# The slot-update tail of a fused attention and slot-routing block: three values products in split form, transposes under a sum, and the first output tiles one place earlier

## What is computed

```
alpha = softmax of the 8 largest routing logits of a row, 0 elsewhere   # [rows, 64]
S_new = gated update of the slots from alpha^T x                          # [64, 512] per sequence
q, k, v = S_new wq + bq, S_new wk + bk, S_new wv + bv
y   = S_new + softmax(q k^T * scale) v
y   = layernorm(y) * ln_g + ln_b
out = x + (alpha (y wvp + bvp)) wo + bo
```

## Time and profile before

| | |
|---|---|
| median of three runs | 371.1 us (370.83 to 371.25) |
| the profiled execution's own time | 370.99 us |
| its span, first to last instruction | 369.1 us |
| mean granted clock of TensorE | 0.997 |
| busy: PE, DVE, ACT, POOL | 350.7, 243.5, 188.2, 194.1 us |
| output tiles | 32 transfers of 256 KB, issued from 340.95 to 365.02 us |

### The profile page before, as it was taken

The page is one execution under the profiler, slowest core; times in us unless marked ns, Lnnn a source line. Parts: engine busy times, 40 slices in busy tenths (PEclk is TensorE's granted clock), DMA queues, the critical chain, the costliest instruction groups (busy, mean ns, idle before and its releaser), DMA issues.

```text
span 369.1 us, 6877 instructions
## 1 busy us (share of the span) xinstructions
PE 350.7 (95%) x2250; PEld 273.4 (74%) x2250; DVE 243.5 (66%) x718; ACT 188.2 (51%) x394; POOL 194.1 (53%) x344
## 2 busy tenths in 40 slices
PE   5999999999999999999999999999999999999881
PEld 2475658999998898898988989867556785657651
DVE  0839986877788787787887786765372433366673
ACT  1260035568669577587496594665232342244541
POOL 1317056888776786677678568440021151215882
PEclk9999999999999999999999999999999999999998
DMA  5889966242232312323131100079000000000778
GB/s 170 271 290 365 387 175 189 72 115 90 83 115 61 113 60 86 88 62 111 59 115 59 31 2 2 0 233 315 3 0 0 2 0 0 3 0 0 282 299 330
DMA packets 41366, 42.78 MB, mean 116 GB/s; under 512 B 3678, under 2 KB 32478, under 8 KB 41331
## 3 DMA queue, kind: packets, MB, share of 16 engines
q1 hardware_dynamic: 39376, 40.42, 33.1%
q10 hardware_dynamic: 1666, 1.27, 1.2%
q0 software_dynamic: 288, 0.66, 0.7%
HBM read 32.18 MB, written 8.39 MB: 110 GB/s over the span
## 4 chain that ended last, share of the span: by engine, by line
PE 72%; DVE 10%; POOL 6%; issue 4%; ACT 4%; DMA 3%; SPq 0%; DVEq 0%; POOLq 0%; ACTq 0%
PE psum L328 11%; PE psum L329 10%; PE psum L330 10%; PE psum L1344 8%; PE psum L1394 5%; PE psum L1554 4%; PE psum L1597 3%; PE psum L1240 3%; PE psum L1422 3%; PE psum L1615 2%; PE psum L1282 2%; DMA WvpT<-in_WvpT 2%; PE psum L1375 2%; PE psum L1541 2%; POOL X L474 2%
## 5 line engine op out<-in xcount | busy, mean ns | idle before, releaser
L328 PE MATMUL psum<-GW_hi,hT_hi 128*128 128x292 f32 (+1 forms) x256 | 79.0, 308 | 1.1 <-POOL GW_lo L456 1.0
L330 PE MATMUL psum<-GW_lo,hT_hi 128*128 128x292 f32 (+1 forms) x256 | 74.0, 289 | 0.0
L329 PE MATMUL psum<-GW_hi,hT_lo 128*128 128x292 f32 (+1 forms) x256 | 73.9, 288 | 0.0
L474 POOL TENSOR_TENSOR X<-X,th 128x512 f32<-128x512 f32 x32 | 38.3, 1196 | 31.5 <-ACT th L1062 31.5
L328 PEld LDWEIGHTS psum<-GW_hi,hT_hi 128*128 128x128 f32 x256 | 48.4, 189 | 2.9 <-issue 2.0
L469 POOL TENSOR_TENSOR hT_lo<-xT,hT_hi 128x512 fp32r<-128x512 f32 x32 | 43.4, 1356 | 11.9 <-ACT hT_hi L1018 11.9
L329 PEld LDWEIGHTS psum<-GW_hi,hT_lo 128*128 128x128 f32 x256 | 48.3, 189 | 0.2 <-issue 0.2
L330 PEld LDWEIGHTS psum<-GW_lo,hT_hi 128*128 128x128 f32 x256 | 48.1, 188 | 0.0
L328 PE MATMUL psum<-xhT_hi,w_hi 128*128 128x256 f32 x128 | 38.4, 300 | 0.1
L329 PE MATMUL psum<-xhT_hi,w_lo 128*128 128x256 f32 x128 | 36.1, 282 | 0.0
L330 PE MATMUL psum<-xhT_lo,w_hi 128*128 128x256 f32 x128 | 36.0, 282 | 0.0
(11 more groups left out here) (247 smaller groups left out, 820.6 us busy)
## 6 DMA issues: line engine op xcount, KB each, us to landing
X<-in_x SPq DMA_DIRECT2D x32, 256.0 KB, 3.5
xT<-in_xT SPq DMA_DIRECT2D x32, 256.0 KB, 2.7
out<-ost SPq DMA_DIRECT2D x32, 256.0 KB, 2.8
WhhT<-in_WhhT SPq DMA_DIRECT2D x1, 3072.0 KB, 12.5
WihT<-in_WihT SPq DMA_DIRECT2D x4, 768.0 KB, 7.8
WvpT<-in_WvpT SPq DMA_DIRECT2D x4, 256.0 KB, 5.5
Wo<-in_wo ACTq DMA_DIRECT2D x4, 256.0 KB, 3.7
WaT<-in_WaT SPq DMA_DIRECT2D x1, 1024.0 KB
```

The lines of the kernel that those rows point to most:

```text
L328: pe.matmul(out, w_hi, m_hi, start=start, stop=False)
L329: pe.matmul(out, w_lo, m_hi, start=False, stop=False)
L330: return pe.matmul(out, w_hi, m_lo, start=False, stop=stop)
L474: pool.tensor_tensor(tile_x(r), tile_x(r), halves(th[:, :]), ALU.add).then_inc(S("x2"), 1)
```

## The change

The values of pairs 1 to 3 are computed with `mm3` from split halves: `Wv_hi`, `Wv_lo` (2048 columns each) and `SnT_hi`, `SnT_lo` (128 x 4 x 384). ACT makes the upper halves, DVE the lower ones. They lie over the gate weights `WihT` and under the buffers of `SV_hi`, `SV_lo`, `al_hi` and `al_lo`, so ACT's first cast waits for the late gates, and `high_alpha` now waits for the last values product. In `y_of` the slots are turned back by four true transposes, put ahead of the attention product and its waits. `values(3)` is cut in two around `y_turned(0)`. `low_y` of pairs 0 and 1 goes from DVE to POOL. PE runs outs 0 and 1 ahead of `values_of(1)`, outs 2 and 3 behind it, and `y_turned(3)`, `values_of(2)`, outs 4 and 5, `values_of(3)`, and the rest follow. From outs 6 on, three pairs of banks are used in turn. Tile 2 goes from POOL to DVE. Two pairs of semaphores early in the kernel become one each; nothing else changes there.

```diff
+    Wv_hi = place("Wv_hi", [P, KC, D], F32R, "v1")       # v1: over WihT, same start as c1
+    Wv_lo = place("Wv_lo", [P, KC, D], F32R, "v1")
+    SnT_hi = place("SnT_hi", [P, KC, VN], F32R, "v1")
...
-        return OB2[m % 2]
+        return OB2[m % 2] if m < 6 else OB2[(2, 0, 1)[m % 3]]
...
-        return n % 3 == 2
+        return n > 4 and n % 3 == 2
...  POOL
-        low_alpha(0)
-        low_alpha(1)
         scales_y(0)
         scales_y(1)
+        low_y(0)
         scales_y(2)
+        low_alpha(0)
+        low_y(1)
         low_slot_values(0)
         scales_y(3)
         low_y(2)
+        low_alpha(1)
         low_slot_values(1)
-        out(2)
+        out(5)
         low_y(3)
-        out(5)
         low_alpha(2)
+        low_slot_values(2)
         out(8)
         out(11)
-        low_slot_values(2)
-        out(14)
+        low_slot_values(3)
         low_alpha(3)
-        out(17)
-        low_slot_values(3)
-        for n in range(20, NT, 3):
+        for n in range(14, NT, 3):
...  DVE
+        low_values_weight()
         late_new_slots()
+        low_slots(V1, EN, 2)
+        low_slots(EN, SLOTS, 3)
         scores(0, EP, 1)
...
+        stats_y(2)
         weights_turned(EP, NPAIR, 2)
-        low_y(0)
-        stats_y(2)
         norm_y(2)
-        low_y(1)
         slot_values(0)
         stats_y(3)
+        outs(0)
         norm_y(3)
+        outs(1)
         slot_values(1)
-        for m in range(6):
-            outs(m)
+        outs(2)
+        outs(3)
+        outs(4)
         slot_values(2)
-        for m in (6, 7):
-            outs(m)
+        outs(5)
         slot_values(3)
...  ACT
         def high_alpha(g):
-            act.wait_ge(S("gi_late"), 3)
+            act.wait_ge(S("v"), NPAIR)
...
+        high_values_weight()
         act.wait_ge(S("gn_in"), KC + 1)
...
+        high_slots(V1, EN)
         query_key(0, EN, 0)
+        act.wait_ge(S("snt"), KC + 1)
+        high_slots(EN, SLOTS)
         exps(0, EP, 1)
-        high_alpha(0)
-        high_alpha(1)
         query_key(EN, SLOTS, 2)
         exps(EP, NPAIR, 2)
+        high_alpha(0)
         turned_y(0)
         turned_y(1)
+        high_alpha(1)
         high_slot_values(0)
         turned_y(2)
         high_slot_values(1)
-        scaled_out(2)
+        scaled_out(5)
         turned_y(3)
-        scaled_out(5)
         high_alpha(2)
+        high_slot_values(2)
         scaled_out(8)
         scaled_out(11)
-        high_slot_values(2)
-        scaled_out(14)
+        high_slot_values(3)
         high_alpha(3)
...  PE
+                    last = mm3(pe, VB[g], SnT_hi[:, k, at_g], SnT_lo[:, k, at_g], Wv_hi[:, k, :], Wv_lo[:, k, :],
+                               k == 0, k == KC - 1)
...
-            pe.matmul(yb, atT[:, g, :], V[:, g, :], start=True, stop=True)
             for c in range(KC):
-                last = pe.matmul(yb[:, c * P:(c + 1) * P], SnT[:, c, g * P:(g + 1) * P], ident[:, :],
-                                 start=False, stop=c == KC - 1, skip_group_check=True)
+                pe.matmul(yb[:, c * P:(c + 1) * P], SnT[:, c, g * P:(g + 1) * P], ident[:, :], start=c == 0, stop=False,
+                          is_transpose=True, skip_group_check=True)
+            pe.wait_ge(S("atT"), 1 + g // EP)
+            pe.wait_ge(S("vs"), g + 1)
+            pe.matmul(yb, atT[:, g, :], V[:, g, :], start=False, stop=True, skip_group_check=True).then_inc(S("y"), 1)
...
-        values(3)
+        values(3, 0, 2)
         y_turned(0)
+        values(3, 2, KC)
...
         y_turned(2)
-        values_of(1)
         outs(0)
         outs(1)
+        values_of(1)
+        outs(2)
+        outs(3)
         y_turned(3)
-        for m in (2, 3, 4, 5):
-            outs(m)
         values_of(2)
-        outs(6)
-        outs(7)
+        outs(4)
+        outs(5)
         values_of(3)
-        for m in range(8, NT // 2):
+        for m in range(6, NT // 2):
             outs(m)
```

More of the change, by code:

```diff
@@ L103, in program @@
     blockmask = place("blockmask", [P, P], F32, "b1")
+    V1, VN = P, SLOTS - P
+    region("v1", cursor["x"])
+    Wv_hi = place("Wv_hi", [P, KC, D], F32R, "v1")
+    Wv_lo = place("Wv_lo", [P, KC, D], F32R, "v1")
+    SnT_hi = place("SnT_hi", [P, KC, VN], F32R, "v1")
     region("c1", cursor["x"])
@@ L177, in program @@
     alT = place("alT", [P, NPAIR * TPB, P], F32, "keep")
+    region("v2", cursor["keep"])
+    SnT_lo = place("SnT_lo", [P, KC, VN], F32R, "v2")
     region("c4", cursor["keep"])
@@ L278, in program @@
     YT = (banks[0], banks[1], banks[0], banks[0])
-    OB2 = ((banks[2], H0), (banks[1], H1))
+    OB2 = ((banks[2], H0), (banks[1], H1), (banks[0], SI))
     def out_banks(m):
-        return OB2[m % 2]
+        return OB2[m % 2] if m < 6 else OB2[(2, 0, 1)[m % 3]]
     def out_tile(n):
@@ L530, in low_y @@
             pool.wait_ge(S("yhi"), g + 1)
-            pool.wait_ge(S("ylo"), g)
             pool.tensor_tensor(ynT_lo[:, g % 2, :, :], ynT[:, g % 2, :, :], ynT_hi[:, g % 2, :, :].bitcast(F32),
@@ L644, in _ @@
         v.wait_ge(S("encWT"), KC)
-        v.wait_ge(S("gall"), 1)
+        v.wait_ge(S("gauss"), 2)
         with v.If(f > 0):
@@ L652, in _ @@
                 v.wait_ge(S("u_out"), i + 2)
-        v.tensor_copy(flagf[:, :], anyv[:, 0:1]).then_inc(S("u_done"), 1)
+        v.tensor_copy(flagf[:, :], anyv[:, 0:1]).then_inc(S("first_row"), 1)
         stats1(0)
         v.wait_ge(S("pre"), HB_DONE)
-        v.tensor_tensor(hb[:, :], banks[0][:, 0:HC], b1, ALU.add).then_inc(S("hb"), 1)
+        v.tensor_tensor(hb[:, :], banks[0][:, 0:HC], b1, ALU.add).then_inc(S("first_row"), 1)
         link(v.tensor_tensor(brz[:, 0:2 * KC], bih[:, 0:2 * KC], bhh[:, 0:2 * KC], ALU.add), "rt")
@@ L674, in _ @@
         stats1(2)
-        v.wait_ge(S("gw"), 1)
+        v.wait_ge(S("gauss"), 1)
         link(v.tensor_scalar(gw[0:WP, :], gw[0:WP, :], geo[:, 1:2], None, ALU.max), "rt")
@@ L919, in norm_y, with low_values_weight, low_slots @@
             v.wait_ge(S("yn"), g + 1)
[L921 to L924, removed]
+        def low_values_weight():
+            v.wait_ge(S("vhi"), 1)
+            v.tensor_tensor(Wv_lo[:, :, :], Wv[:, :, :], Wv_hi[:, :, :].bitcast(F32), ALU.subtract).then_inc(S("vlo"), 1)
+        def low_slots(lo, hi, n):
+            v.wait_ge(S("vhi"), n)
+            at_s = slice(lo - V1, hi - V1)
+            v.tensor_tensor(SnT_lo[:, :, at_s], SnT[:, :, lo:hi], SnT_hi[:, :, at_s].bitcast(F32),
+                            ALU.subtract).then_inc(S("vlo"), 1)
         def slot_values(g):
@@ L999, in _ @@
         act.wait_ge(S("dist"), 2)
-        act.activation(gw[0:WP, :], wcl[0:WP, :], ACT.Exp, scale=-1.0 / DEV).then_inc(S("gw"), 1)
+        act.activation(gw[0:WP, :], wcl[0:WP, :], ACT.Exp, scale=-1.0 / DEV).then_inc(S("gauss"), 1)
         link(act.activation(gall[:, :], gall[:, :], ACT.Exp, scale=-1.0 / DEV))
-        act.mul(gall[:, :], gall[:, :], 1.0 / T).then_inc(S("gall"), 1)
+        act.mul(gall[:, :], gall[:, :], 1.0 / T).then_inc(S("gauss"), 1)
         act.wait_ge(S("in_wa"), 16)
@@ L1191, in high_alpha, with high_values_weight, high_slots @@
             act.copy(al_hi[:, g % 2, :, :], alT[:, TPB * g:TPB * (g + 1), :]).then_inc(S("al_hi"), 1)
+        def high_values_weight():
+            act.wait_ge(S("in_v"), 48)
+            act.wait_ge(S("gi_late"), 3)
+            act.copy(Wv_hi[:, :, :], Wv[:, :, :]).then_inc(S("vhi"), 1)
+        def high_slots(lo, hi):
+            act.copy(SnT_hi[:, :, lo - V1:hi - V1], SnT[:, :, lo:hi]).then_inc(S("vhi"), 1)
         def scaled_out(n):
@@ L1220, in _ @@
         high_slot_values(1)
-        scaled_out(2)
+        scaled_out(5)
         turned_y(3)
-        scaled_out(5)
         high_alpha(2)
+        high_slot_values(2)
         scaled_out(8)
         scaled_out(11)
-        high_slot_values(2)
-        scaled_out(14)
+        high_slot_values(3)
         high_alpha(3)
-        scaled_out(17)
-        high_slot_values(3)
-        for n in range(20, NT, 3):
+        for n in range(14, NT, 3):
             scaled_out(n)
@@ L1259, in _ @@
         last.then_inc(S("pre"), 1)
-        pe.wait_ge(S("gall"), 1)
+        pe.wait_ge(S("gauss"), 2)
         pe.wait_ge(S("flag"), 1)
@@ L1274, in _ @@
                 pe.sem_inc(S("u_read"), 1)
-        pe.wait_ge(S("u_done"), 1)
+        pe.wait_ge(S("first_row"), 1)
         pe.wait_ge(S("encWT"), KC)
@@ L1286, in _ @@
         pe.wait_ge(S("wcs"), 2)
-        pe.wait_ge(S("hb"), 1)
+        pe.wait_ge(S("first_row"), 2)
         pe.matmul(banks[0], cmean[:, :], wcs[:, :], start=True, stop=True).then_inc(S("pre"), 1)
@@ L1548, in scores, with values @@
             last.then_inc(S("ss"), 1)
-        def values(g):
+        def values(g, lo=0, hi=KC):
             if g > 1:
                 pe.wait_ge(S("vs"), g - 1)
-            for k in range(KC):
-                last = pe.matmul(VB[g], SnT[:, k, g * P:(g + 1) * P], Wv[:, k, :], start=k == 0, stop=k == KC - 1)
-            last.then_inc(S("v"), 1)
```

(24 more changed lines are left out.)

2 lines of the change are left out of this document (removed).

## The result

The changed kernel takes 373.96 us, median of four runs (373.71 to 374.05); the kernel before, beside it, 371.12 (370.83 to 371.25). The ratio is 1.0077, 95% interval [1.0059, 1.0094]: slower by 0.8%. The profiled execution took 373.9, with a span of 372.1 and a mean granted clock of 0.986. The direction and the place are as predicted. The time is 1.6 us above the forecast of 372.4, since one term of the sum was sized wrong: it lies outside the 371.8 to 373.3 that the forecast gave its own case, and inside the whole range, 370.0 to 374.0, by 0.04. That it still lies inside is luck.

What follows compares the result with a forecast made beforehand. The prediction took SP's in-order output queue, standing at POOL's tile 8, as the bound: 351.55 + 0.96 lead + 24 tiles at 0.64 (15.35) + 1.0 hole + 1.66 + 1.89 = 372.4 us. Range 370.0 to 374.0.

Steps and rivals of the forecast that it cites:

- its own case: Whole kernel: in-order queue behind tile 8 sets the end, 372.4 us, range 371.8 to 373.3, chance 0.49.
- What bounds the kernel: Output drain: the tile POOL finishes at which SP's queue stands last, plus 0.64 us for each tile behind it.
- the same sum: End of kernel: SP's issue time, 0.96 us lead, 0.64 per remaining tile, 1.66 from dry queue to span end.
- PE sets the end: Rival for the kernel's end: all 3.6 us of saved PE work come through, 367.4 us; chance 0.17.
- The savings on PE: PE: split values save 0.6 us for each of three pairs, transposes 0.44 in each of four; 3.6 in all.
- the rival in which these forms give nothing: Values and turned slots on PE: products stay 3.43, turns 0.89, 374.8 us; shares 0.08 with two other rivals.
- The split halves were hidden: Making the halves on ACT and DVE early: cost taken as zero; without cover, under 1 us.
- The added wait: PE ahead of `values_of(0)`: `high_alpha(0)` holds back `turned_y(0)` on ACT, so start is 330.5, only 0.8 earlier than before.
- The order on POOL: `low_slot_values(2)` now ahead of tile 8, so tile 8 is finished at 351.5, against SP's issue at 348.53 before.
- Tile 14's hole: Output drain: tile 14 reaches SP at 356.4, transfers run dry once, adding 1.0 us.
- `values_of(0)` at 2.82: PE's twelve f32r products for pair 0's slot values: taken at 2.82 us, as in the kernel before.
- this rival, at 2.8 us: PE's wait before `values_of(0)` drops TensorE's clock to 1.2 GHz: 2.8 us more, 375.2; shares 0.08 with two others.

Runs made afterwards that it cites:

- e1: Changed kernel with ACT's cast `high_alpha(0)` moved behind `turned_y(0)`; 370.58 us, ratio 0.9987 to the kernel before.
- e2: Changed kernel with two f32 products that nobody reads added on PE inside its wait ahead of `values_of(0)`; 372.16 us, ratio 1.0023 to the kernel before.
- e6: Changed kernel with the values of pairs 1 to 3 in plain f32 again, without split halves; 371.71 us, ratio 1.0012 to the kernel before.
- e7: Changed kernel with slots turned back by plain f32 products against the identity instead of transposes; 372.63 us, ratio 1.0041 to the kernel before.
- e9: e7 with two more casts of pair 0's `alT` on ACT, so PE waits longer; 375.32 us, ratio 1.0099 to the kernel before.
- e10: Changed kernel, transposes kept, with `low_y(0)` on DVE again; 371.42 us, ratio 1.0012 to the kernel before.
- e12: Changed kernel with tile 8 alone finished by DVE; 371.99 us, ratio 1.0029 to the kernel before.
- e3: Changed kernel with tiles 8 and 14 finished by DVE instead of ACT and POOL; 371.31 us, ratio 0.9983 to the kernel before.
- e8: Kernel before with only the transposes in `y_of`, put ahead of the attention product; 369.57 us, ratio 0.9955 to the kernel before.
- e4: e1 with tiles 8, 11 and 14 finished by DVE; 367.79 us, ratio 0.9916 to the kernel before.
- e5: Kernel before with only `low_slot_values(2)` moved ahead of tiles 8 and 11 on POOL; 372.75 us, ratio 1.0042 to the kernel before.

## Why the prediction was right, and where it was off

**What bounds the kernel: right.** The end follows from SP's issue of tile 14 in the changed kernel, to 0.1 us. With the issue times of the table the same sum gives the spans of e1, e2, e6, e7, e9, e10 and e12 to 0.1 as well. Moving tiles 8 and 14 to DVE (e3) gives 2.3 us back with `values_of(0)` as slow. The rival "PE sets the end" (367.4) falls: e2 and e6 add work to PE and are faster. PE's work counts as far as it brings those tiles forward, as in e8. The third pair of banks, tile 2 on DVE and PE's new order of outs were given nothing, and no run takes one of them alone; e4, which keeps all three, is faster than the kernel before.

**The savings on PE: right in size.** Two pairs' values took 5.65 (5.64), and four transposes 0.44 from one start to the next piece's (319.45 to 319.89; 0.45 in the sum). So the rival in which these forms give nothing falls too. The split halves were hidden, as taken: by the timelines PE's values of pair 1 started between 311.24 and 311.69 in the runs that have the halves, and between 311.42 and 311.68 in those without, so no cost of theirs shows.

**The added wait: right.** Pair 0's rows came to PE at 324.47 (forecast 324.2) after a wait of 0.65 (0.6), and `values_of(0)` began at 330.71 (330.5). e1 shows that the place of `high_alpha(0)` on ACT makes the wait: moved behind `turned_y(0)`, it leaves 0.46. With `low_y(0)` back on DVE and the cast left in its place (e10), 1.74 of the 2.35 remain.

**The order on POOL: right.** e5 prices it alone, 1.5 us on the kernel before. Tile 14's hole came as well, forecast at 1.0: the transfers' share in the stretch at 358 is 0.16.

**The term that was off: `values_of(0)` at 2.82.** It measured 4.41, at 1.2 GHz for most of its length. Start 0.2 late and 1.6 longer: tile 8 at 353.23 in place of 351.5, tile 14 at 358.00 in place of 356.4, and the end moved by the same 1.6. The prediction did name this rival, at 2.8 us, and turned it down because the earlier trace rows show the clock near whole for some time after PE's last work at the end. That row did not carry over to this wait. Nor was the rival's size right: the first products still ran at the full clock and so did the last, so that 1.6 was lost and not 2.8; in e9, where the clock fell before PE began, it was 5.26 - 2.83 = 2.4. Mechanism and rival did not exclude each other, as the list of cases treated them: both happened.

**Is it the wait or the transposes?** In PE-mode transpose (Part 4) of TensorE: Matmul & The Clock Gate, the Trainium skill has it that a transpose doesn't count as busy for the gate the same way. The runs here don't need that rule: the clock falls in e9 without the change's transposes, and with them it stays whole in e10 (wait 1.74) and e2 (0.64 behind filling products). Ahead of `values_of(0)` the profiled runs sort by the length of the wait: whole at 1.89 and less, fallen at 3.20, and at 2.35 fallen twice and whole once. But the length of one wait is not all that decides. Late in e5 PE stood for 1.43 us (until 356.67), worked for 1.0 and stood for another 0.40, and the clock fell too, once it had resumed:

```profile
355.00:356.00 1.00, 0.23 (x4) 0.00 (x0) 0.75 (x1) 0.17 (x1) 1.00 (x2) 1.00 1.07 410
356.00:357.00 1.00, 0.34 (x3) 0.35 (x5) 0.51 (x1) 1.00 (x2) 0.94 (x2) 1.00 1.04 404
357.00:358.00 1.00, 0.64 (x6) 0.20 (x2) 0.90 (x2) 0.26 (x2) 1.00 (x2) 1.00 1.05 404
358.00:359.00 1.00, 0.96 (x6) 0.65 (x6) 0.57 (x1) 0.46 (x1) 1.00 (x2) 0.71 1.06 412
359.00:360.00 1.00, 1.00 (x6) 0.64 (x6) 0.75 (x2) 0.34 (x1) 1.00 (x2) 0.50 1.05 402
```

What decides at 2.35 stays open, and so does whether transposes shift that edge, since no pair of runs had equal waits around it with and without them.

**Transfers: right.** The stretches from 359 to 370 moved 395 to 416 GB/s. The prediction's 410 to 414 is the upper end in its own trace: the stretches between the two that it shows moved 397 to 404. That shifts its sum by under 0.1, since the lead was taken as the remainder of the same drain. The page DMA: Bandwidth & Descriptors of the Trainium skill (Specifications) gives an HBM limit of about 358 for each core, as half of what a stack gives to two. This core's output ran above that.

## What to carry to other kernels

When outputs leave through one in-order queue, look up which engine finishes the tile at which that queue stands, and what stands ahead of that tile on that engine: one line moved on POOL cost 1.5 us here (e5), and the new order on POOL, with one cast on ACT ahead of urgent work and the clock lost behind it, more than undid 3.6 us of work saved on PE. On an in-order engine, an instruction that waits for a late resource belongs behind the urgent ones that wait for nothing. And when work is taken away ahead of a wait, the wait can grow, so look at the granted clock behind it: ahead of `values_of(0)` it held at 1.89 us and not always at 2.35. e4 keeps the change's savings and mends the order, and is 0.8% faster than the kernel before.

## What the runs showed of the hardware that was not expected

- Behind a single stand of PE of 2.35 us the clock was lost in two of three profiled runs, and in the changed kernel the fall showed only after PE had resumed (330.71; whole until 331, 0.57 in the stretch at 331). At the end of the kernel before, the granted clock was still 0.93 in the stretch at 366, with PE's last work in the one at 361.
- Two plain products whose result nobody reads (1.88 us) made the kernel 1.8 us faster (e2).
- POOL's two subtractions of 256 columns took 2.40 in the changed kernel and 1.40 in the one before. DVE's subtraction of 2048 columns ran beside them (304.77 to 307.06). In e6, the changed kernel without that subtraction and ACT's casts, they took 1.40 again. The delay was hidden, as the start of PE's values shows.
